# Edge counts of a graph layer on TensorE: the ring of one-hot pairs is cut into single pairs, and the loops run in rounds of two pairs, later of one

## The reference

```python
deg = segment_sum(ones, edge_dst); deg_inv = 1 / max(deg, 1)
msg = h[edge_src]
agg = segment_sum(msg, edge_dst)
layer = h @ W_self + (agg * deg_inv[:, None]) @ W_neigh + b
```

## Time and profile before

| what | value |
|---|---|
| time before, median of three runs | 1321.35 us (1321.3 to 1321.87) |
| span of the profiled execution | 1319.4 us |
| what lies around the span (median less span) | 1.95 us |
| TensorE matmul busy | 1314.5 us, 100% |
| VectorE busy | 879.3 us, 67% |
| ScalarE busy | 475.0 us, 36% |
| granted TensorE clock | 1.000 |

### The profile page before, as it was taken

One profiled execution on the slowest core, in us unless ns is written; L12 is line 12 of the kernel. 1 busy time (PEld: TensorE's weight loads), 2 busy tenths in 40 slices (PEclk: granted clock), 3 DMA queues, 4 the chain that ended last, 5 costly groups with the idle time before them and its releaser, 6 DMA issues.

```text
span 1319.4 us, 19208 instructions
## 1 busy us (share of the span) xinstructions
PE 1314.5 (100%) x6490; PEld 627.2 (48%) x6490; DVE 879.3 (67%) x1526; ACT 475.0 (36%) x709; POOL 3.8 (0%) x16
## 2 busy tenths in 40 slices
PE   9999999999999999999999999999999999999999
PEld 5454445555445444444444444444444444444444
DVE  7854542352677767767879858855877567886774
ACT  7765565355213233321211112210000076464460
POOL 0000000000000000000000000000000000000000
DMA  8487886765044541014766864645545409723523
GB/s 351 147 281 265 272 274 227 296 212 181 24 158 156 181 145 48 17 27 139 207 179 194 227 176 159 223 156 199 179 151 175 131 30 296 144 56 96 128 54 107
DMA packets 173196, 219.93 MB, mean 167 GB/s; under 512 B 93889, under 2 KB 127425, under 8 KB 171841
## 3 DMA queue, kind: packets, MB, share of 16 engines
q1 hardware_dynamic: 132992, 209.00, 48.4%
q10 hardware_dynamic: 40128, 9.97, 4.4%
HBM read 164.41 MB, written 32.51 MB: 149 GB/s over the span
## 4 chain that ended last, share of the span: by engine, by line
PE 99%; DVE 1%; DMA 0%; issue 0%; ACT 0%; DVEq 0%
PE ps L1749 54%; PE ps L2000 13%; PE ps L2088 9%; PE ps L2125 9%; PE ps L1880 8%; PE ps L1947 2%; PE ps L1888 1%; PE ps L1801 1%; PE ps L1783 1%; DMA XIN<-in_x 0%; DVE Zb L1013 0%; PE ps L2170 0%; PE ps L1770 0%; DVE st L977 0%; DVE XH L1008 0%
## 5 line engine op out<-in xcount | busy, mean ns | idle before, releaser
L1749 PE MATMUL ps<-S,XH 128*128 128x512 f16 x2400 | 526.6, 379 | 0.0
L1749 PEld LDWEIGHTS ps<-S,XH 128*128 128x128 f16 (+1 forms) x2400 | 234.3, 98 | 277.3
L2000 PE MATMUL ps<-Zb,AT 128*128 128x512 f16 x800 | 175.4, 379 | 0.0
L2000 PEld LDWEIGHTS ps<-Zb,AT 128*128 (+1 forms) x800 | 78.2, 98 | 94.1
L1749 PE MATMUL ps<-S,Zb 128*128 128x512 f16 x480 | 106.4, 379 | 0.0
L1880 PE MATMUL ps<-XH,S 128*128 128x512 f16 (+1 forms) x576 | 102.6, 339 | 0.0
L1749 PE MATMUL ps<-Zb,XH 128*128 128x512 f16 x432 | 94.8, 379 | 0.0
L1274 DVE TENSOR_SCALAR STREAM<-tables,keys 128x320 f16 x240 | 71.4, 298 | 25.5 <-issue 13.2
L1395 DVE SCALAR_TENSOR_TENSOR STREAM<-STREAM,cols 128x1024 fp8e4<-128x1024 f32 x64 | 79.2, 1278 | 0.0
L1880 PEld LDWEIGHTS ps<-XH,S 128*128 128x128 f16 x576 | 56.1, 98 | 47.0 <-issue 2.3
L1749 PEld LDWEIGHTS ps<-S,Zb 128*128 128x128 f16 x480 | 47.0, 98 | 54.4 <-issue 0.6
(11 more groups left out here) (248 smaller groups left out, 1422.9 us busy)
## 6 DMA issues: line engine op xcount, KB each, us to landing
STREAM<-in_w1t SPq DMA_DIRECT2D x64, 512.0 KB, 5.0
STREAM<-in_w2t SPq DMA_DIRECT2D x52, 512.0 KB, 4.4
STREAM<-in_w_all SPq DMA_DIRECT2D x48, 512.0 KB, 5.3
XIN<-in_x SPq DMA_DIRECT2D x20, 512.0 KB, 5.3
SPLIT<-in_Wneigh SPq DMA_DIRECT2D x16, 512.0 KB, 5.8
SPLIT<-in_Wself SPq DMA_DIRECT2D x16, 512.0 KB, 4.4
w1q_scratch<-STREAM SPq DMA_DIRECT2D x16, 512.0 KB, 5.0
w2q_scratch<-STREAM SPq DMA_DIRECT2D x16, 512.0 KB, 3.7
```

Source lines behind the costliest of these rows:

```text
L1749: last = mm(acc[:, n * BANK:(n + 1) * BANK], left(l, kc), right(kc, r)[:, n * BANK:(n + 1) * BANK], start=(kc == 0 and i == 0), stop=(kc = ...
L2000: last = mm(banks(bank + n, 1), AT_tile(t, s), Z[:, r, s, n * BANK:(n + 1) * BANK], start=(s == 0 and r == 0), stop=(s == NT - 1 and r == 1))
```

## The change

The ring has 16 places of one pair each, in the same bytes as before. A part runs in rounds of `round_of(part)` pairs: two in parts 0 to 5, one in parts 6 to 40. `hot` and `free` count pairs now, so they go up by two or by one a round, and each engine computes the place of a pair from its own count of pairs.

```diff
-RING = 4
+RING = 16
+WIDE_PARTS = 6
...
-        hots = stream16[:, 0:RING * QUAD * (GW + P)].rearrange("p (r n) -> p r n", r=RING)
-        hot_m = [hots[:, :, q * GW:(q + 1) * GW] for q in range(QUAD)]
-        hot_s = [hots[:, :, QUAD * GW + q * P:QUAD * GW + (q + 1) * P] for q in range(QUAD)]
+        hots = stream16[:, 0:RING * (GW + P)].rearrange("p (r n) -> p r n", r=RING)
+        hot_m, hot_s = hots[:, :, 0:GW], hots[:, :, GW:GW + P]
...
+        def round_of(part):
+
+            return 2 if part < WIDE_PARTS else 1
...
-                with dve.Fori(dve.snap(first, min_val=0, max_val=EC), dve.snap(end, min_val=1, max_val=EC + 1), QUAD) as c_:
+                pairs_each = round_of(part)
+                with dve.Fori(dve.snap(first, min_val=0, max_val=EC), dve.snap(end, min_val=1, max_val=EC + 1),
+                              pairs_each) as c_:
                     n = dve.snap(made)
                     dve.reg_alu(slot, made, RING - 1, ALU.bitwise_and)
-                    r = dve.snap(slot, min_val=0, max_val=RING - 1)
-                    dve.wait_ge(S("free"), n + 1)
+                    r = dve.snap(slot, min_val=0, max_val=RING - pairs_each)
+                    dve.wait_ge(S("free"), n + pairs_each)
                     alone(dve)
-                    for j in range(QUAD):
-                        V.tensor_scalar(hot_m[j][:, bass.ds(r, 1), :], iota_m[:, :],
+                    for j in range(pairs_each):
+                        V.tensor_scalar(hot_m[:, bass.ds(r + j, 1), :], iota_m[:, :],
                                         key_m[:, bass.ds(c_ + j, 1)], None, ALU.is_equal)
...
-                    one.then_inc(S("hot"), 1)
-                    dve.reg_add(made, made, 1)
+                    one.then_inc(S("hot"), pairs_each)
+                    dve.reg_add(made, made, pairs_each)
...
-                with pe.Fori(pe.snap(first, min_val=0, max_val=EC), pe.snap(end, min_val=1, max_val=EC + 1), QUAD):
+                pairs_each = round_of(part)
+                with pe.Fori(pe.snap(first, min_val=0, max_val=EC), pe.snap(end, min_val=1, max_val=EC + 1), pairs_each):
                     n = pe.snap(done)
                     pe.reg_alu(used, done, RING - 1, ALU.bitwise_and)
-                    r = pe.snap(used, min_val=0, max_val=RING - 1)
-                    pe.wait_ge(S("hot"), n + 1)
-                    for q in range(QUAD):
-                        one = mm(ps[:, at_:at_ + GW], hot_s[q][:, bass.ds(r, 1), :],
-                                 hot_m[q][:, bass.ds(r, 1), :], start=False, stop=False, skip_group_check=True)
-                    one.then_inc(S("free"), 1)
-                    pe.reg_add(done, done, 1)
+                    r = pe.snap(used, min_val=0, max_val=RING - pairs_each)
+                    pe.wait_ge(S("hot"), n + pairs_each)
+                    for q in range(pairs_each):
+                        one = mm(ps[:, at_:at_ + GW], hot_s[:, bass.ds(r + q, 1), :],
+                                 hot_m[:, bass.ds(r + q, 1), :], start=False, stop=False, skip_group_check=True)
+                    one.then_inc(S("free"), pairs_each)
+                    pe.reg_add(done, done, pairs_each)
```

More of the change, by code:

```diff
@@ L1266, in count_dve @@
                 dve.reg_alu(end, lohi, LO_UNIT - 1, ALU.bitwise_and)
-                with dve.Fori(dve.snap(first, min_val=0, max_val=EC), dve.snap(end, min_val=1, max_val=EC + 1), QUAD) as c_:
+                pairs_each = round_of(part)
+                with dve.Fori(dve.snap(first, min_val=0, max_val=EC), dve.snap(end, min_val=1, max_val=EC + 1),
+                              pairs_each) as c_:
                     n = dve.snap(made)
                     dve.reg_alu(slot, made, RING - 1, ALU.bitwise_and)
-                    r = dve.snap(slot, min_val=0, max_val=RING - 1)
-                    dve.wait_ge(S("free"), n + 1)
+                    r = dve.snap(slot, min_val=0, max_val=RING - pairs_each)
+                    dve.wait_ge(S("free"), n + pairs_each)
                     alone(dve)
-                    for j in range(QUAD):
-                        V.tensor_scalar(hot_m[j][:, bass.ds(r, 1), :], iota_m[:, :],
+                    for j in range(pairs_each):
+                        V.tensor_scalar(hot_m[:, bass.ds(r + j, 1), :], iota_m[:, :],
                                         key_m[:, bass.ds(c_ + j, 1)], None, ALU.is_equal)
-                        one = V.tensor_scalar(hot_s[j][:, bass.ds(r, 1), :], iota_s[:, :],
+                        one = V.tensor_scalar(hot_s[:, bass.ds(r + j, 1), :], iota_s[:, :],
                                               key_s[:, bass.ds(c_ + j, 1)], -float(g * P), ALU.subtract, ALU.is_equal)
-                    one.then_inc(S("hot"), 1)
-                    dve.reg_add(made, made, 1)
+                    one.then_inc(S("hot"), pairs_each)
+                    dve.reg_add(made, made, pairs_each)
             steps(dve, 4, 6, qm_dve)
```

## The result

| | before | after |
|---|---|---|
| median of 4 runs each | 1321.38 us (1321.3 to 1321.87) | 1337.78 us (1335.98 to 1338.56) |
| ratio after to before | | 1.0122, 95% interval 1.0107 to 1.0136 |
| span of the profiled execution | 1319.4 us | 1336.1 us (its run: 1337.9) |

What follows compares the result with a forecast made beforehand. TensorE, busy 1314.5 of 1319.4 us, was taken as the bound. Gaps of 5.6 + 2.4 + 1.7 + 6.0 + 0.9 = 16.6 us, less 5.5 for removed matmuls, gave 11 more: 1332 us, range 1326 to 1339.

Steps and rivals of the forecast that it cites:

- first case: Favoured outcome, chance 0.66: short rounds use up the sequencers' lead over the engines; 1332 us, own range 1328 to 1336.
- leaving a loop: After a loop whose lead is used up, count and branch delay the product: about 0.05 us in 18 parts, 0.9.
- 41 matmuls removed: 240 pairs become 199 on TensorE's array: 41 x 0.135 = 5.5 us saved.
- wide rounds on TensorE's sequencer: Parts 0 to 3, rounds of two pairs at 1.05 us: gaps of 1.4, 2.2, 1.4 and 0.6, sum 5.6 us.
- rounds of one: TensorE's sequencer at 0.80 us a round: six-pair parts 6 to 8 lose 0.7 us each, five-pair parts 0.05; sum 2.4.
- VectorE in tiles 5 to 8: VectorE's rounds of 0.97 us need more than TensorE's time in these tiles; TensorE waits 1.7 us for `hot`.
- the three-part tiles: Tiles 14 to 18, late one-hots: second parts 1.2 us (three times) and 0.4, third parts 0.4 in five tiles; sum 6.0.
- the preparation: TensorE's sequencer, from loading a part's bound to computing its first address: 1.0 us, read from part 1.
- Cheap branches: Rival, chance 0.12: short loops branch back as cheaply as out, rounds cost 0.13 us less; +7.5 us, 1329.
- A longer lead: Rival, chance 0.03: TensorE's queue holds 64, its sequencer's gaps vanish, VectorE's excess rises by some 2 us; 1326.
- faster: Rival, chance 0.05: no round's cost reaches the array, only the removed matmuls count; 1316 us.
- VectorE in earnest: Rival, chance 0.12: VectorE bounds; its other work loses its cover, 1.3 us more in each of five tiles; 1339.

Runs made afterwards that it cites:

- run 4: Kernel before with its own ring and 60 rounds, each round only as wide as its part needs, 205 pairs instead of 240: 1317.41 us, ratio 0.9971.
- run 2: Changed kernel with rounds of four pairs in parts 0 to 5 and of one from part 6 on: 1329.68 us, ratio 1.0067.
- run 6: Changed kernel with bounds rounded up to 240 pairs; VectorE in rounds of two and one, TensorE in rounds of four: 1359.17 us, a single run.
- run 3: Changed kernel with rounds of two pairs in parts 0 to 5 and of four from part 6 on: 1330.28 us, ratio 1.0071.
- run 9: Changed kernel with part 1 alone in rounds of four pairs: 1335.03 us, ratio 1.0105.
- run 1: Changed kernel's ring, but rounds of four pairs in every part, 240 pairs in 60 rounds: 1323.59 us, ratio 1.0019.
- run 7: Changed kernel with the second pair's place taken from a shifted view, without its register operation: 1333.85 us, ratio 1.0095.
- run 8: Changed kernel's ring with rounds of four pairs everywhere and places from shifted views, without the added register operations: 1321.22 us, ratio 1.0001.
- run 5: Changed kernel with bounds rounded up to 240 pairs; TensorE in rounds of two and one, VectorE in rounds of four: 1366.48 us, a single run.

## Why the prediction was right, and where its sum was too small

The forecast of 1332 (1326 to 1339, slower at 0.90) held the sign, the mechanism and the range; the move was 16.4 us instead of 10.6, and the first case's own range of 1328 to 1336 was missed by the median. By the terms of its own sum, with "leaving a loop" taken as 0.13 us in each of the 23 parts that have a gap:

| term | forecast | in the trace |
|---|---|---|
| 41 matmuls removed | -5.5 | -5.6 |
| wide rounds on TensorE's sequencer, parts 0 to 3 | 5.6 | 7.2 |
| rounds of one, parts 6 to 14, and VectorE in tiles 5 to 8 | 2.4 + 1.7 | 3.5 |
| the three-part tiles | 6.0 | 6.5 |
| leaving a loop with an empty stock | 0.9 | 3.0 |
| half clock behind part 1 | none | 1.6 |
| later start of the stage, small differences | none | 0.5 |
| sum | 11.1 | 16.7 |

**The removal** is right, and run 4 has it nearly by itself.

**The wide rounds** are right in kind and in the round's price (1.06 against 1.05). What was mis-sized is the preparation, taken as 1.0 us from one part. Part 1 took 1.0; parts 0, 2 and 3 took 1.3 to 1.6, since the load of the bound alone took up to 0.9 us instead of 0.3. The trace of the kernel before had this already: its longest load took 0.90 us, in part 3, where the preparation was 1.6. All loads of the bound, and part 2's:

```profile
L1940 PEldq TENSOR_LOAD <-bnd x41: 297/302/902, 356.2 to 600.6; - x41
...
L1940 PEldq TENSOR_LOAD <-bnd x1: 836/836/836, 385.1 to 385.1; - x1
```

The median is 302 ns, the longest 902 (part 13). Where the lead of 3.9 us is spent to the end, each tenth of it comes out as gap. Against this the time from the last address to its matmul was 0.23 us (wide) and 0.13 (single), not 0.3. The six longest loads (0.55 to 0.90 us, parts 2, 3, 11, 13, 15 and 17) all ran while the core's DMA engines moved 268 to 400 GB/s, and 30 of the 35 others ran while they moved nothing. But part 5's load took 0.30 us at 232 GB/s and part 0's 0.50 at none, so the cause is not shown.

**The rounds of one** cost 0.835 us, not 0.80, which with the shorter way to the matmul gives about the forecast gaps in parts 6 to 8. (Parts with five pairs are five, 9 to 12 and 14, where the prediction counted six; that is worth 0.05 us.) **VectorE in tiles 5 to 8** was wrong: 1.7 us were forecast, and the profile puts every wait of TensorE in parts 6 to 14 down to its own sequencer (2.1 us in five waits). Instead parts 9 and 11, with five pairs, have gaps of 0.52 where about 0.1 was forecast. The load of part 11's bound took 0.55 us. Part 9 is the one place where VectorE shows: its load took 0.30 us, but its first address stands 1.28 us behind the load's start instead of 0.98, just behind the end of the part's first one-hot (441.44 + 0.25 = 441.69).

```profile
441.44 0.25 DVE L1282 TENSOR_SCALAR STREAM<-tables,keys 128x128 f16 x1
...
L1954 PEldq FUSED_REGOPS  x1: 74/74/74, 441.7 to 441.7; - x1
```

So 0.3 us of the 1.7 came. The total of the two terms is near only because the one made up for part of the other.

**The three-part tiles** behave as described: the gaps are 1.05 to 1.20 us in parts 25, 28, 31 (forecast 1.2), 0.43 in part 34 (0.4), and 0.34 to 0.42 in three of the third parts (0.4). Without the 0.13 us for leaving the loop, which has its own row, these seven are each 0.1 to 0.3 below the forecast. Two third parts, 29 and 38, show 1.26 and 1.31. The row's total is near only because 29 and 38 are 0.7 to 0.8 above theirs. VectorE's timeline at part 29, with part 28's last two rounds ahead of it:

```profile
548.65 0.30 DVE L1280 TENSOR_SCALAR STREAM<-tables,keys 128x320 f16 x1 [0.49 <-issue]
...
549.62 0.30 DVE L1280 TENSOR_SCALAR STREAM<-tables,keys 128x320 f16 x1 [0.50 <-PE ps L1954]
...
551.10 0.30 DVE L1280 TENSOR_SCALAR STREAM<-tables,keys 128x320 f16 x1 [1.01 <-PE ps L1954]
...
552.61 0.30 DVE L1280 TENSOR_SCALAR STREAM<-tables,keys 128x320 f16 x1 [0.71 <-issue]
...
553.82 0.30 DVE L1280 TENSOR_SCALAR STREAM<-tables,keys 128x320 f16 x1 [0.68 <-PE ps L1954]
```

Part 28's rounds are 0.97 us apart as forecast, part 29's 1.5 and 1.2. ("PE" as releaser is only the last semaphore seen; the idle time is the sequencer's.) Why is open too; run 2 has the same in part 25.

**Leaving a loop** was mis-sized most: a product that follows an empty stock starts 0.26 to 0.27 us behind the last matmul (426.35 to 426.61, 536.92 to 537.19) instead of 0.135, so 0.13 a part and not 0.05, and in 23 parts. (The prediction said 18, but its own terms name gaps in 21.)

**The half clock** was not in the sum at all. The Trainium skill, "TensorE: Matmul & The Clock Gate", Part 1 on the clock gate, names 1.2 and 2.4 GHz as the two states of TensorE's clock; the prediction drew on this page for the queue's depth only. The trace agrees with these two levels: granted clock 0.52 over 376.90 to 380.40, and 1.00 on both sides. Four runs of the change gave three at 0.999 and one at 1.000 (1335.98, 1.7 to 2.6 us below the others), so the median carries it.

**The rivals.** *Cheap branches* is ruled out: the round measured 0.835 and 1.06, not 0.67 and 0.92. *A longer lead* and *faster* are ruled out by the array's gaps behind "issue" in part 1. The Trainium skill's depth of 64 for TensorE's queue, in the table at the top of "TensorE: Matmul & The Clock Gate", does not show here. The prediction made an estimated 6.9 us of lead from it, and in none of the 41 parts, before or after, does the load of the bound stand more than 3.9 us ahead of the part's first matmul. *VectorE in earnest* (1339) is nearest in time and wrong in cause: its mark, more than 1.5 us of waits a tile in tiles 5 to 9, is absent; its mechanism appears only in run 6, where VectorE makes 240 pairs in short rounds. The range held because it was carried by the 1339 of this rival, not because the terms were well sized: that is luck.

## What to carry to other kernels

A loop whose bounds are in registers has a price per round on each engine's sequencer (here 0.84 us on TensorE and 0.97 on VectorE for one pair, 0.135 us on the array), and it is free only while the stock in front of it lasts; count rounds, not just the work in them, and take out work by fitting the width of a round to its part, as run 4 does, rather than by making rounds shorter. Give places inside a round as fixed offsets of a view: each computed one costs a register operation of 0.1 us where the stock is gone. Work a preparation out from its longest case in the trace, not from one instance, when the margin behind it is a few tenths.

## What was not expected of the hardware

- Behind some 2.4 us of gaps, none longer than 0.55 us, in a stage otherwise full, TensorE was granted half its clock for about 3.5 us, which cost 1.64 us. It comes run by run: in three runs of four of the changed kernel, two of four of run 3, one of four of runs 2 and 9, in none of the runs of 1, 4, 7 and 8. The single executions of runs 5 and 6, with more idle time, had three and four such stretches. What sets it off was not settled: taking away part 1's gap (run 9) did not take it away for good.
- The load of one bound into a register took 0.30 us in most parts and up to 0.90 us in a few, the six longest all while DMAs were moving data (but so did one of 0.30 us).
- VectorE's round of one took 0.97 us in most parts and 1.2 in some, with the same operations.
- A wait that the profile named after VectorE stood 11 us behind the one-hots it was said to wait for (part 2).
